# A graph network on one core: the message's lower part moved from VectorE to GpSimd, a fourth tile of target one-hots made by VectorE

## Time and profile before

| what | value |
|---|---|
| median of three runs | 7416.02 us |
| profiled execution, its own time | 7420.97 us |
| span of the profiled execution | 7419.4 us |
| PE, DVE, ACT, POOL busy, share of the span | 77%, 71%, 40%, 37% |
| mean granted TensorE clock | 0.857 |

### The profile page before, as it was taken

How to read it: one execution, slowest core, us unless ns; L and a number is a source line. 1 busy time by engine, 2 the same in 40 slices (tenths; PEclk the granted TensorE clock), 3 DMA queues, 4 the chain that set the end, 5 groups by cost and what they waited for, 6 DMA issues and landing times. The chain is left out here.

```text
span 7419.4 us, 276961 instructions
## 1 busy us (share of the span) xinstructions
PE 5700.9 (77%) x87510; PEld 4679.5 (63%) x87511; DVE 5283.6 (71%) x15345; ACT 2935.0 (40%) x5054; POOL 2776.7 (37%) x4280
## 2 busy tenths in 40 slices
PE   4888888864666557677677677776989998999776
PEld 3666666643444447667677677676866776777676
DVE  7555545568999968878788788788865554555698
ACT  2444444433444444334344344343743332333343
POOL 2676666754333225445355355353000000000254
PEclk9888888875555579989899899898769998999999
DMA  2666666652222368778588588686531111111497
GB/s 75 179 185 176 177 172 180 179 140 50 73 73 73 89 212 223 197 183 224 154 225 224 151 224 223 158 226 169 200 139 63 63 63 46 63 63 63 112 236 201
DMA packets 1403296, 1098.84 MB, mean 148 GB/s; under 512 B 1012405, under 2 KB 1171820, under 8 KB 1393466
## 3 DMA queue, kind: packets, MB, share of 16 engines
q1 hardware_dynamic: 887994, 797.65, 35.5%
q0 software_dynamic: 224768, 240.90, 13.4%
q10 hardware_dynamic: 290304, 57.05, 4.4%
HBM read 815.28 MB, written 278.78 MB: 147 GB/s over the span
## 5 line engine op out<-in xcount | busy, mean ns | idle before, releaser
L544 POOL DMA_DIRECT2D big<-rows x2592 | 1418.9, 547 | 3320.1 <-issue 2348.5
L1295 PE MATMUL ps<-big 128*128 128x64 bf16 x41472 | 1917.7, 193 | 660.3 <-DVE big L1809 278.7
L1295 PEld LDWEIGHTS ps<-big 128*128 128x128 fp8e4 x41472 | 1683.8, 98 | 740.5 <-issue 726.3
L1307 PE MATMUL ps<-big 128*128 128x64 bf16 x20736 | 1731.8, 194 | 15.1 <-issue 8.9
L814 POOL DMA_INDIRECT rows<-big x800 | 1025.2, 1281 | 609.4 <-issue 356.3
L1307 PEld LDWEIGHTS ps<-big 128*128 128x128 bf16 x20736 | 1067.9, 98 | 25.3 <-issue 18.8
L1018 ACT CAST big<-big 128x512 bf16<-128x512 f32 x720 | 445.4, 619 | 944.6 <-DVE big L1809 944.6
L1586 DVE SCALAR_TENSOR_TENSOR big<-big 128x1000 f32<-128x1000 f32 (+1 forms) x300 | 359.8, 1199 | 590.6 <-ACT big L905 432.3
L1212 PEld LDWEIGHTS ps<-big 128*125 128x125 f32 (+1 forms) x4800 | 693.6, 215 | 101.9 <-issue 58.5
L1255 PE MATMUL ps<-identb,big 128*128 128x128 bf16 x2304 | 472.3, 308 | 360.5 <-DVE big L1697 359.0
L1024 ACT CAST big<-big 128x512 bf16<-128x512 f32 x864 | 534.1, 618 | 454.3 <-issue 334.8
(11 more groups left out here) (263 smaller groups left out, 9369.7 us busy)
## 6 DMA issues: line engine op xcount, KB each, us to landing
big<-ohsD SPq DMA_DIRECT2D x432, 512.0 KB, 3.8
big<-ohdD SPq DMA_DIRECT2D x432, 320.0 KB, 4.4
big<-rows POOLq DMA_DIRECT2D x2592, 32.0 KB, 3.8
big<-rows SPq DMA_DIRECT2D x2592, 32.0 KB, 3.6
big<-maskD SPq DMA_DIRECT2D x50, 1600.0 KB, 6.7
big<-rows ACTq DMA_DIRECT2D x1728, 32.0 KB, 3.6
big<-keyT SPq DMA_DIRECT2D x100, 488.3 KB
maskD<-big SPq DMA_DIRECT2D x25, 1600.0 KB, 6.2
```

Of the source, the lines that this page charges most:

```text
L544: eng.dma_start(edge[:, s.r, j, :], rows[bass.ds(v[s.r * (hi - lo) + j - lo], P), col]).then_inc(landed[s.r], 16)
L1295: last = pe.matmul(pG[g.r][:, j * D:(j + 1) * D], ohsR[:, g.r, at:at + P].bitcast(F8), slices[:, g.r, q, (3 * k + c) * D:(3 * k + c + 1) * D],
L1307: last = pe.matmul(pacc[:, bass.ds(w[j], D)], hot[:, g.r, j * P:(j + 1) * P], parts[:, g.r, c, j * D:(j + 1) * D], start=False, stop=False ...
```

## The change

GpSimd now makes the lower part, with the same operation on the same data, after the loads of each step; VectorE no longer does. In the last four steps GpSimd has no loads and only the lower parts. KEEP falls from 5 to 4, so MADE grows from 3 to 4: one tile less of each group's target one-hots is stored and loaded, and L1781 makes 128x512 in place of 128x384.

```diff
-KEEP = 5
+KEEP = 4
 MADE = GT - KEEP
...
                     load_edges(pool, v, s, *POOL_SHARE, col, edge_pooled)

+                def lower(s):
+                    if s.live(4):
+                        g = s.lag(4)
+                        pool.wait_ge(mid_ready, base + g.i + 1)
+                        hold(pool)
+                        pool.tensor_tensor(parts[:, g.r, 2, :], res[:, g.r % 2, :], parts[:, g.r, 1, :], ALU.subtract).then_inc(lo_ready, 1)
+
...
                     for r in range(U):
                         one(Step(t, r), v)
+                        lower(Step(t, r))
+                for i in range(NG, NG + 4):
+                    lower(Step(i // U, i % U))
...
-            def lower(s, base):
-                if s.live(4):
-                    g = s.lag(4)
-                    dve.wait_ge(mid_ready, base + g.i + 1)
-                    dve.tensor_tensor(parts[:, g.r, 2, :], res[:, g.r % 2, :], parts[:, g.r, 1, :], ALU.subtract).then_inc(lo_ready, 1)
-
...
                     rest(s, l * NG, "edge")
-                    lower(s, l * NG)
                     remake(s, l * NG)
...
                     rest(s, base, kind)
-                    lower(s, base)
                     remake(s, base)
```

## The result

Median of four runs 7606.52 us (7600.05 to 7612.24), against 7420.35 us (7408.58 to 7446.19) for the kernel before on the same occasions: ratio 1.0235, 95% interval [1.0217, 1.0252]. A second set of four gave 7595.76 against 7418.98 us, 1.0265 [1.0198, 1.0332]. The forecast was 7555 us. The profiled execution took 7612.24 us, with a span of 7610.6. Of the 31 later runs of the kernel before, one took 9148.57 us at a granted clock of 0.547; the ratios leave it out.

A forecast was written before the change was run, and what follows sets the result against it. VectorE, TensorE and DMA were taken to bound the step jointly at 3.06 us; with turns VectorE's 2.96 plus waits gives 3.22, so 115 + 27 = +142 us on 7416, said as 7555 us; range 7290 to 7860.

The forecast's parts named there:

- turns: Edge passes: VectorE's copies, residual and one-hots exclude GpSimd's operation, making VectorE's cycle 2.96 us instead of 2.15; 7555 us, chance 0.42.
- Own work of VectorE, 2.15 us: VectorE's cycle per step in the passes: 2.62 less 0.60 for the lower part plus 0.13 for the fourth tile.
- GpSimd's operation, 1.03 us: Price of GpSimd's new 128x512 operation per step: upper bound 1.03 us, two streams one after the other; lower bound 0.56.
- GpSimd's cycle, 2.80 us, its sequencer running ahead: GpSimd per step: 1.65 for DMAs, 1.03 operation, 0.12 gap, if its sequencer prepares DMAs while the cores work.
- The rival with 3.58 us: GpSimd becomes the bound: its sequencer doesn't run ahead, 3.58 us a step, 7886 us; 7650 to 7890, chance 0.19.
- The layout: Where VectorE stalls: the residual 0.73 us in three steps of four, the one-hots 1.03 us in the table-load step.
- The waits at the message, +0.26: VectorE's idle time before the message: 0.16 us for TensorE stays, 0.10 of 0.24 for rows; step 3.22 us.
- The base: Today's layer-pass step: VectorE 2.6, TensorE 2.8 and DMA 2.6 us lie close together, their jitter making 3.06.
- The faster rival: No turns are taken: VectorE at 2.15 us is out of it, step some 2.95 us, -85 us, 7330; chance 0.30.
- Loads covered, the one-hots' stage unchanged: Row loads, issued about three steps ahead, still land in time; the stage storing the one-hots stays within 10 us.
- The scatter isn't later: GpSimd finishes the lower part 2.3 us after the residual, VectorE some 3 us after, so TensorE's scatter isn't delayed.
- the second rival: GpSimd the bound, chance 0.19; signs: POOL idle only for the table load, TensorE waiting for GpSimd's line.

The follow-up runs named there:

- 8-column kernel: GpSimd's operation cut to 8 of its 512 columns, the rest of the lower part left out, against the changed kernel: 7395.95 us, 0.9952 of the kernel before.
- non-additive experiments: Against the kernel before, each half of the change by itself: lower part on GpSimd with KEEP 5, 7451.41 us; KEEP 4 with lower part on VectorE, 7393.96 us.
- lower part alone: Changed kernel with KEEP back at 5: GpSimd makes the lower part, VectorE one-hots of three tiles; 7451.41 us, 1.004 of the kernel before.

## Why the prediction was right, and where it wasn't

The sign, the size and the cause of the loss were right: 7606 us for 7555 (+190 us for +142), inside the case's own range of 7450 to 7680, by turns between GpSimd's operation and VectorE's. The steps:

- **Own work of VectorE, 2.15 us**: right. The 8-column kernel has 2.23 us of busy time a step, where the kernel before had 260.83/98 = 2.66 by the same count; the difference of 0.43 is near the forecast's 0.47.
- **GpSimd's operation, 1.03 us**: 1.17 in the median, 1.22 in the mean of the stretch. The upper bound, taken for the value, was too low. The 1.12 us estimated from the Trainium skill (GPSIMD Engine Reference, "Elementwise — side-by-side cycle accounting") was closer.
- **GpSimd's cycle, 2.80 us, its sequencer running ahead**: right. Its three DMAs follow an operation without a gap, and two operations with three DMAs between them stand 2.72 us apart at the closest (3002.42, 3005.14). The rival with 3.58 us is out: 90 steps, and GpSimd idle 23.4 us for ScalarE.
- **Turns, 0.81 us a step**: right in kind and in which operations take part, low in size: 0.99 over the span. The layout, 0.73 at the residual in three steps of four and 1.03 at the one-hots in the fourth, was wrong: the copies took 319 of 859 us, and though I had them take turns, my layout charged them nothing.
- **The waits at the message, +0.26**: wrong. They went to 0.02 us (2.1/90): while VectorE is the bound, rows and TensorE are in time. VectorE's cycle came to 297.38/90 = 3.30 us instead of 2.96, and so the sum was nearly right through two errors against each other, 0.34 more in the cycle and 0.24 less in the waits. That is luck, and part of why 7555 lies so near.
- **The base, "three resources lie close together and their jitter makes 3.06"**: wrong, and the worst of the errors. SP's list of issues, 3.05 us, was the bound in the layer passes. (The 0.2 us for semaphores in TensorE's 2.8 us has no row behind it, and no run tests the 2.8.) I had listed what every engine was busy with, and SP, never busy, not at all. The 0.47 us that VectorE gets back were therefore worth 0.03 (the 8-column kernel). The faster rival, 7330 us with a chance of 0.30, could not have come: with no stall whatever the time is 7396.
- **Loads covered, the one-hots' stage unchanged**: right ("DMA big<-rows" 1.6 us; 806.85 us for 806.01).
- **The scatter isn't later**: right in the median, where the lower part is ready 2.6 us after the residual for 3.6 before, but not in every step: it is up to 6.1 us for 5.2, and it is now TensorE's largest wait, one of the signs that I had named for the second rival. With VectorE full it cost nothing that shows; in the 8-column kernel the same wait is 23.2 us and the loss is gone.

```profile
PE ps L1305 <- POOL big L871: 40.9, 44, 2.8
```

With the floor at 3.03 the non-additive experiments make sense. Busy time a step, held part included, against the unheld 2.23 (four tiles) or 2.10 (three):

| kernel | unheld | held | sum | step |
|---|---|---|---|---|
| 8 columns | 2.23 | 0 | 2.23 | 3.03 |
| lower part alone | 2.10 | 0.89 | 2.99 | 3.06 |
| change | 2.23 | 1.07 | 3.30 | 3.33 |

Held time below 3.03 - 2.10 = 0.93 us is free; the lower part alone stays just inside; its 0.4% may be what leaks, which no run shows. The fourth tile adds 0.13 us of work to a VectorE already full, and 0.18 of held time on top. The first follows from the count. Of the second the traces show where it falls. In the changed kernel 147 copies are held from beside a DMA through the operation, each for some 0.8 us more than the operation lasts, 0.14 us a step as an estimate; with the lower part alone no copy took over 1.68 us. And the message, which isn't held, covers 0.19 us of the operation for 0.23. Why copies come to stand there only with the fourth tile I can't show: GpSimd's list (1.17 + 1.61 us, more with the offsets) and VectorE's nearly fill the same step, so it may hang on how their phases fall, and no run varied the phase by itself.

Also open in part is why one stored tile less brings 0.5% while SP's list has the same number of loads. Its issues aren't faster (337 ns in both), but SP waits less for TensorE in the same stretch, 5.1 us before and then

```profile
SPq L469 <- PE ps L1295: 2.1, 6, 0.8
```

The layer passes go at 3.03 us a step for 3.04, the last at 2.89 for 2.92: some 18 us of the 31 by which the profiled spans differ. The rest lies outside the passes, where the spans of other runs differ by as much. Why TensorE frees the buffers sooner no run shows. And fewer row loads on SP (two, with three each on GpSimd and ScalarE), the direct attack on the floor, wasn't tried.

## What to carry to other kernels

Before pricing a relief of one engine, read the waits of every sequencer, those that only issue DMAs above all: one that never waits, as SP in the layer passes here, is the bound, and no busy share shows it. An elementwise operation moved to GpSimd isn't taken off VectorE when VectorE's neighbours read two SBUF tensors or copy: here 1.0 us of a 1.2 us operation came back as longer VectorE instructions, more than the 0.6 us it had cost there. And two edits that are each harmless against a floor (+0.4%, -0.5%) can together rise above it (+2.35%).

## What the runs showed of the hardware beyond what I expected

- A 0.25 us copy took up to 2.25 us: it started beside a DMA of GpSimd's, 0.9 us ahead of the tensor operation, and ended 0.13 us behind it. Of 1728 copies, 147 met such a sequence. DMAs alone held none: beside them no copy of this kernel or the one before took over 0.36 us. Why a copy ahead of the operation waits for it is open.
- Beside GpSimd writing alone, a two-input VectorE operation kept its length (681 ns) and a copy did not (349 ns, up to 2480).
- GpSimd's row loads behind a tensor operation ran back to back, 1.61 us for three, where they took 1.80 before: the sequencer's register work for them ran while the operation was under way (at 3002.75 and 3003.38, beside the operation of 3002.42).
- A 32 KB row load costs SP's sequencer 0.56 to 0.57 us with its register work, as much as it costs GpSimd's cores (0.53 to 0.55), so handing loads to SP is no cheaper here.
- SP went through the same list about 1% faster on two other chips (11.93 us a round without waits for 12.08), enough to move a floor that SP sets.
